# Graph network kernel on one core: x loaded in the first phase, attention sums moved to the tile tables, norm and window counts joined with the features of three blocks

## The chip, the cores and the metric

One core of one Trainium2 chip. The metric is the device time of one execution in microseconds (us); the lower the better. The profile is one execution of its own.

## The reference, cut to what matters

The input is x (3750 nodes by 256), a list of 63750 edges sorted by destination, with a source and one of 8 types each.

```python
h = maximum(layernorm(x), 0)
feat_all = einsum('ni,rhid->rnhd', h, conv_weights)      # 8 types, 4 heads, 64 columns
el = sum(feat_all[type, src] * attn_l[type], -1)         # one number for each edge and head
er = sum(feat_all[type, dst] * attn_r[type], -1)
e = leaky_relu(el + er)                                  # softmax of e over the edges of one destination
x = x + segment_sum(alpha * feat_all[type, src], dst) + h_bias
h = maximum(layernorm(x), 0)                             # then an input layer, and three layers of
h = relu(mean_over_neighbours(h) @ W_agg + h @ W_self + b_hid)
x = x + h @ W_out + b_out
```

## The kernel before, in words

All matrices are cut into blocks of 128 nodes (30 blocks) and chunks of 512 nodes (8 chunks). The program is a row of phases. Each phase is a `with nc.Block()` in which every engine has its own list of instructions, written out by hand, with semaphores between them; at the end of a phase all engines meet, and at some ends GpSimd also clears the semaphores of the phase (`end_phase`, L131). So no engine starts on a phase before the slowest list of the one before is through. SP's list holds most of the transfers, and is worked off in its order: a `wait_ge` in it holds back all that stands behind.

The phases that the change touches, in order:

- **Lists** (L325 to L388). SP loads the four edge lists (12 transfers), ACT's queue loads the attention vectors and the convolution weights (18 transfers), GpSimd and VectorE (DVE) set constants, and DVE turns the lists into numbers (L385).
- **Ends and checks** (L396 to L460, then a sort that is skipped for sorted edges). DVE decides whether the edges are sorted.
- **Tile tables** (`tile_tables`, L613). DVE works out what each group of 128 edges needs (L630 to L669), TensorE (PE) turns it, GpSimd makes masks (L691 to L697), ACT packs pairs of a code and a column for each edge into `pack` (L717, L719), and SP stores them as `pair_tab` (L708). A second copy of the phase is skipped here.
- **Counts** (L740). DVE compares the edges' codes with the starts of 240 windows of 16 nodes (L749 to L752), PE adds the hits up (L812 to L818), and DVE makes `edge_i` of the sums, the first edge of each window (L771 to L805). GpSimd makes 12 row masks beside it (L827 to L838), SP stores them (L857). SP also loads all of x into `x_all` (L844, L846), whose last rows DVE has zeroed (L743), and four small vectors (L848 to L851).
- **Attention and norm** (L889). DVE and GpSimd multiply the weights by the attention vectors (L914, L932) and DVE sums the products to `wlr` (L918). Then come the 8 chunks of the norm: DVE's statistics and scaling (L870 to L882), PE's turning (L972) and products with `wlr` (L961), ACT's relu (L948, L949), DVE's keeping of the results in `elr` (L897). SP meanwhile loads the pairs of the windows of ten blocks with `load_pairs`, and behind them stores `er_tab` (L988).
- **Windows and features** (from L1469). For each of 30 blocks PE makes 7 or 8 windows of the count matrix `a_tab` (three products each, L265, of operands that DVE makes at L254 and L255) and four feature products of 512 columns (each of four matmuls, L1325). ACT takes both out of PSUM (L273 and L1181, L1183); SP stores the windows (L279), ACT's queue the features (L1187). Of the 235 windows with nodes in them, block b takes `BLOCK_W[b]`. SP loads the pairs of block b + 10 ahead of the stores of block b, until all are loaded.

After that come the edge phase (gathers of features, about 530 to 1250 us) and the three layers (to the end). Neither is changed.

The load that matters in the prediction reads where each window begins from `edge_i`, which the counts phase has written:

```python
regs = starts_held[0:many]
sp.load(regs, edge_i[0:1, bass.ds(first, many)])
...
for k, at in enumerate(edge_starts(sp, FIRST_W[b], BLOCK_W[b])):
    sp.dma_start(pairs_in[:, FIRST_W[b] + k, :, :]...)
```

Of the kernel before, what the change touches and what calls it, by code (L numbers as in the profile page):

```python
# [23 lines left out]
FP32 = mybir.dt.float32  # L24
# [42 lines left out]
BLOCK_W = [NREAL * (b + 1) // NBLK - NREAL * b // NBLK for b in range(NBLK)]  # L67
# [32 lines left out]
def gnn_kernel(nc, x, src, dst, etype, conv_w, attn_l, attn_r, h_bias, w_in, b_in, w_agg, w_self,  # L100
               b_hid, w_out, b_out, out):
    ctx = ExitStack()
    with ctx:
        gat = ExitStack()
# [88 lines left out]
        rel = sb("rel", [P, 8, DEPTH])  # L193
        edge_i = sb("edge_i", [1, NTW], I32)
        lo_i = sb("lo_i", [1, NTW], I32)
        past_i = sb("past_i", [1, NTW + 1], I32)

# [41 lines left out]
        def shift_codes(dve, b):  # L239
# [7 lines left out]
            dve.wait_ge(s_rel, b + 1)  # L247
# [32 lines left out]

        def when(eng, flag):
# [27 lines left out]
        s_ld, s_xl, s_at = [nc.alloc_semaphore(a) for a in ("vectors_loaded", "all_x_loaded", "weights_in")]  # L309
        lists_i = stg[:, 5000:5000 + CQ + NTW].bitcast(I32)  # L310
        prod = [stg[:, 4096 + 2048 * i:4096 + 2048 * (i + 1)] for i in range(2)]

        def hrow(i):
            return hT[:, :, :].rearrange("p k n -> p (k n)")[:, i * T:(i + 1) * T].rearrange(
                "p (c j) -> p c j", c=CT)
# [7 lines left out]
        attn = [side[:, 2048 * i:2048 * (i + 1)] for i in range(2)]  # L325

        with nc.Block() as block:
            @block.sync
            def _(sp):
                sp.wait_ge(s_pad, 4)  # L330
                for a, buf in zip((dst, dst, src, etype), raw):
# [5 lines left out]
                                 a[E - rest:E].rearrange("(o j) -> o j", o=1)).then_inc(s_rl, 16)  # L337

# [131 lines left out]
        def sort_edges(flag, key_array, other_array):  # L470
# [18 lines left out]
            with nc.Block() as block:  # L489
# [42 lines left out]
                def _(dve):  # L532
                    with when(dve, flag):
                        for v, buf in zip((0, PADSRC, 0), raw_s):
                            dve.memset(buf, v).then_inc(s_z, 1)
# [76 lines left out]

        def tile_tables(c0, c1, flag=None):  # L613
# [11 lines left out]
            with nc.Block() as block:  # L625
                @block.vector
                def _(dve):
                    with when(dve, flag):
# [19 lines left out]
                        for i, to in enumerate((typ_t, dstloc, fidx_i, code_t, col_t)):  # L648
# [6 lines left out]
                            while at < c1 * P:  # L655
# [15 lines left out]
                                at = end  # L671

# [13 lines left out]
                def _(pool):  # L686
                    with when(pool, flag):
# [9 lines left out]
                        c.link(pool.tensor_copy(dst16[:, 0:nc_, :], cut(dstm)))  # L697

# [15 lines left out]
                def _(act):  # L714
                    with when(act, flag):
# [9 lines left out]
        s_w, s_wc, s_ws, s_ri, s_rw, s_xz = (sem("window_steps"), sem("windows_counted"), sem("window_sums"),  # L725
                                             sem("row_masks"), sem("row_masks_stored"), sem("x_zeroed"))
        begun = stg[:, 1792:1792 + CT * NTW].rearrange("p (c w) -> p c w", c=CT)
        PARTS_T = P // GRAIN
        room = hT[:, :, :].rearrange("p k n -> p (k n)")
# [6 lines left out]
        cbx = stg[0:1, 7800:7800 + NS * U].rearrange("p (s t) -> p s t", s=NS)  # L736
        cnx = work[0:1, 8192:8192 + NS * U].rearrange("p (s t) -> p s t", s=NS)
        subs_of = lambda a: a[0:1, 0:NS * U].rearrange("p (s t) -> p s t", s=NS)
        DUP = 14
        with nc.Block() as block:  # L740
            @block.vector
            def _(dve):
                dve.memset(x_all[:, NBLK - 1:32, :], 0.0).then_inc(s_xz, 1)  # L743
# [10 lines left out]
                same_t = stg[0:1, 8704:8704 + 512]  # L754
# [37 lines left out]
                row = stg[0:1, 8704:8704 + spots]  # L792
                below = stg[0:1, 8768:8768 + (NC - 1) * spots].rearrange("p (c j) -> p c j", c=NC - 1)
# [12 lines left out]

            @block.tensor
            def _(pe):
                for g in range(PARTS_T):
                    pe.wait_ge(s_w, g + 2)  # L810
                    for c in range(CT):
                        pe.matmul(PS[0:1, 7, 0:NTW], one_c, ended[:, g, c, :], start=(g == 0 and c == 0),  # L812
                                  stop=(g == PARTS_T - 1 and c == CT - 1))
                for c in range(CT):
                    pe.matmul(PS[0:1, 5, 0:NTW], one_c, ended[:, PARTS_T - 1, c, :], start=(c == 0), stop=(c == CT - 1))
                pe.wait_ge(s_w, PARTS_T + 3)
                for c in range(CT):
                    mm = pe.matmul(PS[0:1, 6, 0:NTW], ones[:, 0:1], begun[:, c, :], start=(c == 0),  # L818
                                   stop=(c == CT - 1))
                mm.then_inc(s_wc, 1)  # L820
# [18 lines left out]

            @block.sync  # L840
            def _(sp):
                sp.wait_ge(s_xz, 1)
                full = NBLK - 1
                sp.dma_start(x_all[:, 0:full, :],  # L844
                             x[0:full * P, :].rearrange("(b p) f -> p b f", p=P)).then_inc(s_xl, 16)
                sp.dma_start(x_all[0:N - full * P, full, :], x[full * P:N, :]).then_inc(s_xl, 16)  # L846
                for buf, v in ((hb_b, h_bias), (bout_b, b_out)):
                    sp.dma_start(buf[:, :], v.rearrange("(o n) -> o n", o=1).to_broadcast([P, F])).then_inc(s_ld, 16)  # L848
                sp.dma_start(bin_c[:, :], b_in.rearrange("(k p) -> p k", p=P),
                             allow_slow_non_contiguous=True).then_inc(s_ld, 16)  # L850
                sp.dma_start(bh_c[:, :, :], b_hid.rearrange("l (k p) -> p l k", p=P),  # L851
                             allow_slow_non_contiguous=True).then_inc(s_ld, 16)
                sp.wait_ge(s_ri, 12)
                at = 0
# [12 lines left out]
        def ln_stats(dve, rows, c, slot, stats_done, var_ready):  # L867

            for b in range(4):
                dve.bn_stats(stats[:, slot, b, :], rows(b)).then_inc(stats_done, 1)  # L870
# [1419 lines left out]
```

## Time and profile before

| | us |
|---|---|
| median of 3 runs | 2076.78 |
| lowest and highest | 2074.4, 2078.51 |
| the profiled execution | 2072.4 |
| its span, first to last instruction | 2070.6 |
| mean granted TensorE clock, as a share of full speed | 0.901 |

Over the span PE is busy 86%, ACT 55%, DVE 52%, GpSimd 25%. The span falls into the setup (to 154.5 us), the windows and features (to 530), the edges (to 1250) and the layers. Times of instructions are counted from the span's start.

In a timeline a row is: start, duration, engine, line, operation, what it writes and reads, count, and in brackets how long the engine was idle before and what ended that. "SPq" and "ACTq" rows are transfers being issued by a queue; their duration is that of issuing, not of moving the data.

### The profile page before, as it was taken

To read this page: it belongs to the slowest core of one execution; us is meant where nothing else is said; L and a number is where in the kernel's file an instruction comes from. 1 tells how busy PE (TensorE), PEld (TensorE's weight loads), DVE (VectorE), ACT (ScalarE), POOL (GpSimd) and SP (SyncE) were. 2 spreads that over 40 slices of the span, in tenths; PEclk is the share of its full clock that TensorE was granted. 3 is DMA by queue.
4 is the path that set the end of the run, shared out by engine and by line. 5 is a ranking of instruction groups with operands and counts; after the bars stand their busy time and mean duration, and the time that the engine had idled before them with its cause. 6 is when DMAs were issued, how large, how long until landed. Compare 5 with 4: busy or idle time off the path is not lost. (4 is left out here: it accounts for less than half of the span.)

```text
span 2070.6 us, 26209 instructions
## 1 busy us (share of the span) xinstructions
PE 1778.8 (86%) x7604; PEld 1236.5 (60%) x7605; DVE 1081.7 (52%) x3126; ACT 1143.4 (55%) x2498; POOL 521.1 (25%) x544
## 2 busy tenths in 40 slices
PE   1159999999497879798797955999989999999998
PEld 1054444444375557565575634777777777877777
DVE  4858888888365676766767535453550000301011
ACT  0034455565387779797787734454545444544442
POOL 2600000000577777777777300000000000000000
PEclk7569999999687789797898887999999999999999
DMA  4314555555655566565665325333324333363432
GB/s 129 82 14 152 171 195 192 181 201 199 202 146 161 152 182 176 153 188 159 171 173 161 101 63 181 99 123 107 110 77 128 113 116 112 98 208 123 135 123 62
DMA packets 285221, 290.67 MB, mean 140 GB/s; under 512 B 88673, under 2 KB 248102, under 8 KB 284806
## 3 DMA queue, kind: packets, MB, share of 16 engines
q1 hardware_dynamic: 235094, 186.23, 29.3%
q0 software_dynamic: 23952, 66.46, 12.1%
q10 hardware_dynamic: 26016, 36.15, 4.8%
q8 instruction: 64, 1.05, 0.2%
q14 instruction: 95, 0.78, 0.1%
HBM read 201.26 MB, written 87.48 MB: 139 GB/s over the span
## 5 line engine op out<-in xcount | busy, mean ns | idle before, releaser
L1141 POOL DMA_INDIRECT work<-feat_tab,fidx_i x499 | 477.6, 957 | 586.0 <-issue 581.2
L2117 PE MATMUL PS<-a_pe,y_hi 128*128 128x512 f32 (+2 forms) x1440 | 556.7, 392 | 33.4 <-ACT a_pe L2014 33.4
L2117 PE MATMUL PS<-a_pe,y_lo 128*128 128x512 f32 (+2 forms) x1440 | 536.7, 379 | 0.0
L2014 ACT ACTIVATE a_pe<-a_in 128x1536 fp32r<-128x1536 f16 (+1 forms) x240 | 329.3, 1376 | 342.7 <-PE PS L2117 329.1
L2117 PEld LDWEIGHTS PS<-a_pe,y_hi 128*128 128x128 f32 (+1 forms) x1440 | 274.0, 190 | 103.1 <-ACT a_pe L2014 35.0
L1210 ACT ACTIVATE work<-work 128x64 f32<-128x64 f32 x1344 | 325.1, 332 | 0.0
L2117 PEld LDWEIGHTS PS<-a_pe,y_lo 128*128 128x128 f32 (+1 forms) x1440 | 274.2, 190 | 55.2 <-issue 6.7
L1385 PE MATMUL PS<-work,stg 128*128 128x260 f32 x1008 | 289.6, 437 | 6.5 <-ACT work L1210 4.6
L1385 PEld LDWEIGHTS PS<-work,stg 128*128 128x128 f32 x1008 | 207.5, 217 | 65.0 <-issue 19.6
L255 DVE TENSOR_SCALAR side<-iota_c,work 128x512 f16<-128x512 f16 x705 | 245.8, 349 | 0.0
L1325 PE MATMUL PS<-wbuf,hT 128*128 128x512 f32 x480 | 226.9, 595 | 0.0
L2221 DVE TENSOR_TENSOR mean<-PS,rdeg 128x1024 f32<-128x1024 f32 (+1 forms) x24 | 27.2, 1135 | 363.3 <-PE PS L2117 363.0
L273 ACT ACTIVATE side<-PS 128x512 f16<-128x512 f32 x235 | 128.7, 595 | 142.0 <-PE PS L265 69.6
L254 DVE TENSOR_SCALAR side<-iota_c,rel 128x128 f16<-128x128 f16 x705 | 176.9, 251 | 49.1 <-PE PS L265 48.3
L265 PE MATMUL PS<-side 128*128 128x512 f16 x705 | 173.6, 381 | 24.6 <-DVE side L255 16.1
L265 PEld LDWEIGHTS PS<-side 128*128 128x128 f16 x705 | 68.3, 98 | 151.2 <-DVE side L255 36.1
L1335 PE MATMUL PS<-er_win,stg 128*128 128x32 f32 x1008 | 134.9, 294 | 22.5 <-ACT stg L1196 22.5
L1335 PEld LDWEIGHTS PS<-er_win,stg 128*128 128x128 f32 x1008 | 129.9, 211 | 26.4 <-ACT stg L1196 24.5
L1325 PEld LDWEIGHTS PS<-wbuf,hT 128*128 128x128 f32 x480 | 91.8, 191 | 75.1 <-issue 57.9
L1181 ACT ACTIVATE stg<-PS 128x512 f32<-128x512 f32 x120 | 72.0, 600 | 43.3 <-PE PS L1325 42.5
L1588 DVE TENSOR_TENSOR work<-work,PS 128x1024 f32<-128x1024 f32 x42 | 51.3, 1221 | 69.1 <-ACT work L1202 69.1
L1579 DVE TENSOR_TENSOR stg<-PS,dstloc 128x512 f32<-128x512 f32 x126 | 86.4, 686 | 1.5
(257 smaller groups left out, 1674.0 us busy)
## 6 DMA issues: line engine op xcount, KB each, us to landing
a_in<-a_tab SPq DMA_DIRECT2D x210, 384.0 KB, 3.2
feat_tab<-stg ACTq DMA_DIRECT2D x120, 260.0 KB, 2.2
a_tab<-side SPq DMA_DIRECT2D x235, 128.0 KB, 1.8
stg<-dst_tab SPq DMA_DIRECT2D x42, 384.0 KB, 4.0
work<-feat_tab,fidx_i POOLq DMA_INDIRECT x499
h_tab<-outs SPq DMA_DIRECT2D x42, 130.0 KB, 2.6
h_tab<-outs SPq DMA_DIRECT2D x8, 520.0 KB, 3.9
stg<-h_tab SPq DMA_DIRECT2D x8, 520.0 KB, 4.1
```

Of the source, the lines that this page charges most:

```text
L254: dve.tensor_scalar(code[:, s, :], iota_c[:, 0:P], rel[:, k, j:j + 1], None, ALU.is_equal)
L255: dve.tensor_scalar(other[:, s, :], iota_c[:, :], pairs_in[:, w, j, 1:2], None, ALU.is_equal).then_inc(built.pair, 1)
L265: pe.matmul(PS[:, BBS[w % len(BBS)], :], code[:, s, :], other[:, s, :], start=(j == 0), stop=(j == DEPTH - 1)).then_inc(built.free, 1)
L273: act.activation(counts[:, w % KEPT_W, :], PS[:, BBS[w % len(BBS)], :], ACT.Copy).then_inc(built.evicted, 1)
L1141: pool.indirect_dma_start(out=ring[:, s, 0:FE], out_offset=None, in_=feat_tab[:, :], in_offset=bass.IndirectOffsetOnAxis(ap=idx, axis=0)). ...
L1210: ins = act.activation(a, a, ACT.Copy, scale=ring[:, s, F + h:F + h + 1])
L1325: mm = pe.matmul(PS[:, cc, :], hT[:, k, b * P:(b + 1) * P], wc[:, k, cc * 512:(cc + 1) * 512], start=(k == 0), stop=(k == K2 - 1))
L1335: mm = pe.matmul(PS[:, ERB, u * RH:(u + 1) * RH], onehotT[:, u * P:(u + 1) * P], er_win[:, :], start=True, stop=True)
L1385: mm = pe.matmul(PS[:, OUTS[j], 0:EXT], onehot[:, t, :], ring[:, j * U + t, 0:EXT], start=(t == 0), stop=(t == U - 1), skip_group_check=True)
L1579: dve.tensor_tensor(onehot[:, q * QT:(q + 1) * QT, :], IOTA_PS.unsqueeze(1).to_broadcast([P, QT, P]), dstloc[:, tiles_of(i, j, q, QT)].uns ...
L2014: act.activation(a_pe[:, load % A_PE, :, 0:n], a_in[:, load % A_IN, :, 0:n], ACT.Copy).then_inc(s_conv, 1)
L2117: mm = pe.matmul(SUMS(ug, n)[:, f, :], y[0:rows_of, kb, f * P:(f + 1) * P], a_pe[0:rows_of, load % A_PE, kb % KB, 0:n], start=(kb == 0 and ...
```

## The change

x is loaded in the first phase behind the lists (`load_all_x`), with the four small vectors; the zeroing of its last rows goes there too. If the edges had to be sorted, x would be loaded again. The attention products and sums become the functions `attention_sums` and `attention_products`, called at the end of DVE's and GpSimd's lists in the tile tables. The index rows move from `hT` to a buffer of their own that is given back after the setup. The counts phase and the norm phase become one. In it DVE does the norm first and then the counts; PE does the norm, four feature products, the sums of the counts, eight feature products more; ACT does the norm and then keeps and stores the 12 feature products (three blocks, `AHEAD`). SP stores `er_tab`, then the row masks, then waits for a new semaphore that DVE raises at the end of the counts, and then loads the pairs of ten blocks. The windows are spread over the other 27 blocks, 8 or 9 each, 87 of them in the first ten.

```diff
+AHEAD = 3
+BLOCK_W = [0] * AHEAD + [NREAL * (b + 1) // (NBLK - AHEAD) - NREAL * b // (NBLK - AHEAD) for b in range(NBLK - AHEAD)]
...
+        def load_all_x(sp, turn=1):
+            sp.wait_ge(s_xz, turn)
+            sp.dma_start(x_all[:, 0:FULL, :], x[0:FULL * P, :]...).then_inc(s_xl, 16)
+            sp.dma_start(x_all[0:N - FULL * P, FULL, :], x[FULL * P:N, :]).then_inc(s_xl, 16)
...
 (first phase, SP, behind the 12 list transfers)
+                load_all_x(sp)
+                for buf, v in ((hb_b, h_bias), (bout_b, b_out)):
+                    sp.dma_start(buf[:, :], ...).then_inc(s_ld, 16)
+                sp.dma_start(bin_c[:, :], ...).then_inc(s_ld, 16)
+                sp.dma_start(bh_c[:, :, :], ...).then_inc(s_ld, 16)
...
 (first phase, DVE)
+                dve.memset(x_all[:, FULL:32, :], 0.0).then_inc(s_xz, 1)
...
 (tile tables, ends of DVE's and GpSimd's lists)
+                    if flag is None:
+                        attention_sums(dve)
...
+                    if flag is None:
+                        attention_products(pool)
...
+        def attention_sums(dve):
+            dve.wait_ge(s_at, 16 * (K2 * R + 2))
+            for i in range(2):
+                dve.tensor_tensor(prod[0], wc[:, 0, :], attn[i], ALU.mult).then_inc(s_pr, 1)
+                dve.wait_ge(s_pr, 3 * i + 1)
+                for k in range(K2):
+                    if k == 1:
+                        dve.wait_ge(s_pp, i + 1)
+                    dve.tensor_reduce(wlr[...], prod[k]..., AX.X, ALU.add).then_inc(s_pr, 1)
+                    dve.wait_ge(s_pr, 3 * i + k + 2)
+
+        def attention_products(pool):
+            pool.wait_ge(s_at, 16 * (K2 * R + 2))
+            for i in range(2):
+                if i == 1:
+                    pool.wait_ge(s_pr, 3)
+                pool.tensor_tensor(prod[1], wc[:, 1, :], attn[i], ALU.mult).then_inc(s_pp, 1)
...
 (the joined phase, DVE: the norm, then the counts)
+                with when(dve, 0):
+                    dve.memset(x_all[:, FULL:32, :], 0.0).then_inc(s_xz, 1)
+                dve.wait_ge(s_xr, 1)
+                ln_stats(dve, x_rows(0), 0, 0, s_bs, s_vr)
+                over_chunks(dve, step)
...
+                dve.sem_inc(s_wd, 1)
...
 (ACT, behind the norm)
+                act.wait_ge(s_ee, NC)
+                for q in range(4 * AHEAD):
+                    keep_features(act, q)
...
 (PE, behind the norm)
+                pe.wait_ge(s_ht, 2 * NC)
+                for cc in range(4):
+                    sum_features(pe, cc)
+                pe.wait_ge(s_ee, NC)
+                (the sums of the counts, as before)
+                for q in range(4, 4 * AHEAD):
+                    sum_features(pe, q)
...
 (SP)
                 sp.wait_ge(s_ld, 16 * 4)
+                sp.wait_ge(s_xl, 32)
+                with when(sp, 0):
+                    load_all_x(sp, 2)
+                    sp.wait_ge(s_xl, 64)
+                sp.sem_inc(s_xr, 1)
...
-                for b in range(EARLY):
-                    load_pairs(sp, b)
-                over_chunks(sp, store)
+                over_chunks(sp, store)
+                sp.wait_ge(s_ri, 12)
+                (12 stores to rm_tab, as before)
+                sp.wait_ge(s_rw, 16 * 3 * H)
+                sp.wait_ge(s_wd, 1)
+                for b in range(AHEAD, AHEAD + EARLY):
+                    load_pairs(sp, b)
                 sp.wait_ge(s_et, 16 * NC)
...
 (windows and features: DVE, PE, ACT and SP)
-                for b in range(NBLK):
+                for b in range(AHEAD, NBLK):
```

## Rows read from the trace of the kernel before

**Rows 1.** By stage: busy PE, PEld, DVE, ACT, POOL; granted clock, DMA share, GB/s.
```profile
83.20:154.50 71.30, 29.08 (x192) 28.14 (x192) 46.47 (x119) 18.47 (x25) 11.11 (x2) 0.62 0.13 11
157.50:530.00 372.50, 362.42 (x1185) 159.94 (x1185) 316.21 (x1438) 203.88 (x475) 0.00 (x0) 0.99 0.56 186
```

**Rows 2.** Timeline of the attention and norm phase, DVE, GpSimd and SP.
```profile
83.22 4.49 POOL L932 TENSOR_TENSOR stg<-wbuf,side 128x2048 f32<-128x2048 f32 x1 [10.26 <-POOLq L740]
83.23 6.63 DVE L914 TENSOR_TENSOR stg<-wbuf,side 128x2048 f32<-128x2048 f32 x1 [3.25 <-PEq L740]
84.76 58.85 SPq L228 DMA_DIRECT2D work<-pair_tab  x78
...
103.62 1.40 DVE L870 BATCH_NORM_STATS2 stats<-work 128x6 f32<-128x256 f32 x4
...
141.35 0.42 DVE L897 TENSOR_SCALAR stg<-PS 128x256 f32<-128x256 f32 x1 [1.36 <-PE PS L961]
143.66 5.61 SPq L988 DMA_DIRECT2D er_tab<-stg  x8
154.49 0.71 DVE L1470 MEMSET outs<- 128x780 f32 x1 [12.72 <-PEq L133]
```

**Rows 3.** Timeline of the first phase.
```profile
1.64 16.92 ACTq L346 DMA_DIRECT2D wbuf<-in_L_gnn_conv_weights  x16
...
8.99 1.01 SPq L336 DMA_DIRECT2D hT<-in_edge_type  x1
15.70 1.43 DVE L385 CAST hT<-hT 128x512 f32<-128x512 int32 x4 [12.14 <-DMA hT<-in_edge_type]
19.02 0.17 DVE L400 COPY small<-hT 128x7 f32<-128x7 f32 x1 [1.89 <-PEq L327]
```

**Rows 4.** Timeline of the tile tables and the counts.
```profile
43.01 0.68 POOL L697 CAST stg<-hT 128x512 int16<-128x512 f32 x1
...
52.10 0.70 DVE L743 MEMSET work<- 128x768 f32 x1 [2.08 <-PEq L625]
...
53.26 6.44 SPq L846 DMA_DIRECT2D work<-in_x  x1
...
60.12 3.24 POOL L832 TENSOR_TENSOR stg<-stg 1x814 f32<-1x814 f32 x1
...
62.00 1.39 DVE L751 TENSOR_SCALAR small<-hT 128x7 f32<-128x7 f32 x1
...
71.73 0.46 DVE L771 TENSOR_SCALAR stg<-PS,small 1x240 f32<-1x240 f32 x1
```

**Rows 5.** DMA engines' busy tenths in 40 slices: 0 to 25 us, then 50 to 75.
```profile
DMA  0029999998899999999999999799999970000000
...
DMA  0000013999999999999999999941000000000000
```

**Rows 6.** SP's pair loads: first and last of one burst, first of the next.
```profile
90.43 0.86 SPq L228 DMA_DIRECT2D work<-pair_tab  x2
...
94.05 0.33 SPq L228 DMA_DIRECT2D work<-pair_tab  x1
...
96.47 0.86 SPq L228 DMA_DIRECT2D work<-pair_tab  x2
```

**Rows 7.** Windows and features: PE's feature matmuls late in the phase.
```profile
499.79 1.45 PE L1325 MATMUL PS<-wbuf,hT 128*128 128x512 f32 x3
...
502.37 1.88 PE L1325 MATMUL PS<-wbuf,hT 128*128 128x512 f32 x4
...
505.39 1.88 PE L1325 MATMUL PS<-wbuf,hT 128*128 128x512 f32 x4
```

**Rows 8.** Windows and features: SP while it still loads pairs.
```profile
278.67 3.98 SPq L228 DMA_DIRECT2D work<-pair_tab  x8
282.69 6.09 SPq L279 DMA_DIRECT2D a_tab<-side  x8
289.94 4.35 SPq L228 DMA_DIRECT2D work<-pair_tab  x8
```

More of the change, by code:

```diff
@@ L103, in gnn_kernel @@
     with ctx:
-        gat = ExitStack()
+        gat, early = ExitStack(), ExitStack()
         def kept(name, shape, dt=FP32):
@@ L742, in _, with x_rows, keep, step @@
             def _(dve):
-                dve.memset(x_all[:, NBLK - 1:32, :], 0.0).then_inc(s_xz, 1)
+                def x_rows(c):
+                    return lambda b: x_all[:, bass.ds(c * 4 + b, 1), :].rearrange("p o f -> p (o f)")
+                def keep(c, slot):
+                    dve.wait_ge(s_el, c + 1)
+                    dve.tensor_scalar(elr[:, bass.ds(c * 4, 4), :, :],
+                                      PS[:, 4 + slot, 0:256].rearrange("p (b i n) -> p b i n", b=4, i=2),
+                                      0.0, None, ALU.add).then_inc(s_ee, 1)
+                def step(c, slot, first, last):
+                    if not last:
+                        ln_stats(dve, x_rows(c + 1), c + 1, 1 - slot, s_bs, s_vr)
+                    if not first:
+                        wait_past(dve, s_tp, c - 1)
+                    ln_finish(dve, x_rows(c), c, slot, s_sd, s_rs, s_hn, hN[:, slot, :, :])
+                    if not isinstance(c, int) or c > 1:
+                        keep(c - 2, slot)
+                with when(dve, 0):
[3 more added lines that the diff above has]
+                over_chunks(dve, step)
+                keep(NC - 2, 0)
+                keep(NC - 1, 1)
                 c = Chain(dve, s_w)
@@ L838, in _ @@
                 c.link(pool.tensor_scalar(cnx, cnx, BIG, None, ALU.mult))
[L840 to L854, printed above, removed]
-                for a, n in ((csx, U + 1), (cbx, U), (cnx, U)):
-                    for h in range(H):
-                        sp.dma_start(rm_tab[:, at:at + n].unsqueeze(0), a).then_inc(s_rw, 16)
-                        at += n
-                sp.wait_ge(s_rw, 16 * 3 * H)
@@ L979, in _ @@
                 halves(NC - 1, (NC - 1) % 2)
+                pe.wait_ge(s_ht, 2 * NC)
+                for cc in range(4):
+                    sum_features(pe, cc)
+                pe.wait_ge(s_ee, NC)
+                for g in range(PARTS_T):
+                    pe.wait_ge(s_w, g + 2)
+                    for c in range(CT):
+                        pe.matmul(PS[0:1, 7, 0:NTW], one_c, ended[:, g, c, :], start=(g == 0 and c == 0),
+                                  stop=(g == PARTS_T - 1 and c == CT - 1))
+                for c in range(CT):
+                    pe.matmul(PS[0:1, 5, 0:NTW], one_c, ended[:, PARTS_T - 1, c, :], start=(c == 0), stop=(c == CT - 1))
+                pe.wait_ge(s_w, PARTS_T + 3)
+                for c in range(CT):
+                    mm = pe.matmul(PS[0:1, 6, 0:NTW], ones[:, 0:1], begun[:, c, :], start=(c == 0),
+                                   stop=(c == CT - 1))
+                mm.then_inc(s_wc, 1)
+                for q in range(4, 4 * AHEAD):
+                    sum_features(pe, q)
             @block.sync
@@ L1484, in _ @@
                 w = 0
-                for b in range(NBLK):
+                for b in range(AHEAD, NBLK):
                     many = BLOCK_W[b]
@@ L1670, in _ @@
                 w = 0
-                for b in range(NBLK):
+                for b in range(AHEAD, NBLK):
                     if b + EARLY < NBLK:
```

195 lines of the change are left out of this document (81 added, 114 removed).

## The prediction

> **What bounds the kernel now.** I read the busy time by stage first. Windows and features run from 157.5 to 530 us with PE busy 362 of 372.5 us at the full granted clock, while DVE has 316 [rows 1]: there PE is the bound, and a feature product taken out gives its whole time back. The setup before is another thing. From 83.2 to 154.5 us no engine is busy for more than 47 of 71 us [rows 1]; it is a row of phases, and each is as long as its longest list. So I read the timeline of that phase next. DVE does the attention sums from 83.23 to 103.6 us and the norm from 103.62 to 141.77 us. SP, beside it, issues the 78 pair loads from 84.76 to 143.61 us and `er_tab` to 149.27 us, and the next phase begins at 154.49 us [rows 2]. The pair loads are as long as all that DVE does there, and are hidden behind it almost exactly. That is the point on which I forecast: the change puts them behind the counts, where nothing hides them.
>
> All steps are in the profiled execution's time. Its run took 2072.4 us (span 2070.6); the median of the runs shown is 4.4 us higher, and I add the sum of the changes to that median.
>
> **1. x in the first phase.** SP has issued its lists at 10.0 us, ACT's queue its weights at 18.6 us, and the next phase begins at 19.02 us [rows 3]. SP now also issues x, which alone took it some 0.4 + 6.44 us, held until about half was moved [rows 4, 5], and four vectors, which I put at 2.6 us (a window store takes 0.76, 6.09 us for eight [rows 8]). Undisturbed SP ends at 19.4 us, 0.8 after ACT: I call the low end +0.9. But the DMA engines are 90% busy until 20 us with lists and weights, and x alone keeps them so for 20 slices of 0.625 us, 12.5 us [rows 5]. If SP or ACT is held until all is moved, the phase ends 12.5 us later. Neither end is likely, since an issue waits for room, not for landing; I take the middle, +6.5. The lists stand ahead of x on its own queue, so I leave DVE's wait for them (to 15.7 us [rows 3]) alone. The Trainium skill (DMA: Bandwidth & Descriptors, section "Issuing engines are not separate DMA queues") says that transfers of all issuing engines interleave on the same 16 engines; taken to its end that is the +12.5 side. The zeroing of 0.70 us leaves the counts [rows 4] and hides behind the 12.1 us for which DVE waits for the lists [rows 3]: -0.6. x was hidden beside the counts before, so its early arrival gives nothing.
>
> **2. Attention beside the tile tables.** DVE's list is the long one of the tile tables: it ends at 50.02 us and the next phase begins 2.08 us later [rows 4]. The attention work is put at the end of that list. Before it took 20.4 us (83.23 to 103.62 [rows 2]), of which DVE waited 4.4 us: the product of 2048 columns took 6.63 us beside GpSimd's of 4.49 us, that is, it ran when GpSimd's was through. Now GpSimd can do its first product early, when its masks are through at 43.69 us [rows 4], while DVE still has L638 to do and all behind it. Would that hide 4.4 us? At 62.00 us a DVE operation on 7 columns took 1.39 us, to the end of a GpSimd operation on 814 that had begun at 60.12 [rows 4]. So GpSimd's early product should hold L638 up for as long as it saves later. I take 0 for the step (the 20.4 us move, none is saved), with -4.4 and +2 for the range. The Trainium skill (SBUF — State Buffer, section "SBUF: two separate sides") says that the two share a port pair as an exclusive lock, held for a whole instruction; without the lock the step would be worth -4.4.
>
> **3. One phase of two.** Between the last step of the counts and the attention product DVE was idle for 3.25 us [rows 2], for the row masks' landing and the meeting of the engines: gone, -3.3. New on DVE and SP is a test of a flag. Two ends of phases with such a test in one take 2.1 us after the tile tables [rows 4]; I take 1.5 us. Together -1.8.
>
> **4. What runs beside what.** GpSimd's 12 row masks ran beside the counts and held DVE up a few times, as above; now they run beside the norm. About 3 us leave the counts and I put 3 us into the norm: 0, with up to +6. PE does four feature products of 1.9 us at full clock (7.5 us) before the count sums; DVE needs those 19 us after it begins the counts (52.72 to 71.73 us [rows 4]), and the sums take PE some 10 us, so it is just in time: 0, up to +4 if the clock is low. ACT's 12 features at 3.0 us each [rows 7] are 36 us, over before SP's loads are. SP's `er_tab` stores, now taken as the norm goes, and the row masks (some 8 us) are over within the counts.
>
> **5. The pair loads.** Within a burst of eight the starts are 3.62 us apart for seven steps, 0.517 us each; to the next burst, after the register loads, it is 2.42 us [rows 6], 1.9 more than a step. The ten blocks now have 87 windows: 87 x 0.517 + 10 x 1.9 = 64.0 us, none of which can begin before DVE has written `edge_i` and raised the last semaphore. Before, from DVE's last step to the next phase was 12.7 us (141.77 to 154.49). Now it is 64.0 us and the end of the phase. From SP's last issue (149.27 us) to 154.49 us were 5.2 us [rows 2]; of these I put 1.3 us down to the landing of `er_tab`, which is long over now, and keep 3.9: 67.9 us. The step costs +55.2. In the windows phase the same loads come at the same pace (eight in 3.98 us [rows 8]), with DMA much busier, so the pace is that of issuing and I expect no gain from calm.
>
> Setup: 6.5 - 0.6 + 0 - 1.8 + 0 + 55.2 = +59.3.
>
> **6. Windows and features.** A feature product is four matmuls of 0.43 us (1.88 us for four less 1.45 us for three [rows 7]). Twelve products are gone: 48 x 0.43 = -20.6. The windows are as many as before. While SP still loads pairs, eight loads and eight stores have a period of 11.3 us (278.67 to 289.94 [rows 8]); PE's block with eight windows has 4 x 3.02 = 12.1 us [rows 7]. With nine windows SP needs 11.3 x 9/8 = 12.7 us and PE 12.1 + 0.6 (three matmuls at a sixth of 3.02 - 1.72 us each) = 12.7: SP comes level, and slips now and then. I take 0.25 us for each of 17 such blocks, +4, between 0 and +12.
>
> **Sum.** 59.3 - 20.6 + 4 = +42.7. The run of the profile would become 2115.1 us, the median 2119.5; I say **2119**. Less than 0.2% (4 us) cannot be told from no change.
>
> **The rivals.** First, a **milder** case: x is moved without holding anyone (+0.9 for +6.5), the early GpSimd product is really hidden (-4.4), and the windows, now denser, cost PE less than its rate, so that 27 blocks at 12.1 us stand in place of 30 (-36 for -16.6). That is 2090. For it speaks that ACT and DVE have room in a block; against it, that PE has none (it is busy for 362 of 372.5 us [rows 1]) and must still do 235 windows: chance 0.12. Second, a **worse** case: x holds the first phase to the end (+6), GpSimd's masks hold up the norm (+6), and SP becomes the bound of 17 blocks (+8): 2139, chance 0.18. Third, the **other side**, by one mechanism: the end of a phase need not hold the others. If PE, DVE and ACT went into the windows as soon as the pairs of the first block had landed, some 6 us of SP's 64 would be in the open and 58 less would be lost: 2061, faster. It decides when less than 21 us of the loads are exposed (64 less 43). Against it stand DVE's 12.72 us of idleness to 154.49 us, ended by the meeting of the phase after SP's last store [rows 2], and the single list in which SP stores windows behind these same loads: chance 0.04. The change may also not do what its words say in step 2, and by my sum it doesn't: the attention work moves to the end of the list that sets the tile tables' length, not into a shadow.
>
> **Numbers.** The forecast has 0.66, milder 0.12, worse 0.18, the other side 0.04. The forecast's own range takes in the steps' ends as they may add up: from 2119 - 5.6 - 4.4 - 4 = 2105 to 2119 + 6 + 2 + 8 = 2135. The 8 in 10 range reaches somewhat into both neighbours: 2097 to 2137. Slower by over 0.2%: 0.94. Within 0.2%, if between the mild case and the last one it meets in the middle: 0.02. Faster: 0.04.
>
> **What would show it.** In the profile after: the first phase ends at 20 to 31 us, L400 tells. The product of GpSimd starts near 50 us (43.7 + 6.5) and L638 waits for it. The last load of the ten blocks is issued some 64 us after DVE's last step of the counts, with every compute engine idle at the end; ten bursts of 8 or 9 at 0.52 us. The windows phase begins near 214 us and lasts some 356 us. The rest keeps its length. Loads at a pace under 0.3 us, or a windows phase that starts while they are issued, would prove me wrong; so would a windows phase under 340 us.

## The result, and the profile after

The change makes the kernel slower: 2131.2 us (median of 4 runs, 2124.33 to 2137.23) against 2075.6 (4 runs, 2073.25 to 2078.51), a ratio of 1.027 with a 95% interval of 1.0242 to 1.0298. Forecast were 2119 us, with a range of 2097 to 2137. The profiled execution took 2130.88 us, its span 2129.0 against 2070.6 before: 58.4 more.

Where the 58.4 us lie is read from where the phases begin. DVE's memset of `outs` opens the windows phase, the start of the last feature matmul closes it (the last number before the semicolon in these two rows of the view of one source line, first before and then after):

```profile
L1325 PE MATMUL PS<-wbuf,hT x480: 592/592/1061, 160.0 to 527.8; 128*128 128x512 f32 x160
...
L289 PE MATMUL PS<-wbuf,hT x480: 592/592/1061, 124.1 to 584.9; 128*128 128x512 f32 x160
```

| | before | after | difference | forecast |
|---|---|---|---|---|
| windows phase begins | 154.49 | 214.12 | +59.6 | +59.3 |
| its length | 373.3 | 370.8 | -2.5 | -16.6 |
| the rest of the span | 1542.8 | 1544.1 | +1.3 | 0 |

The setup came out at the forecast sum, and the windows did not. The timeline of the changed kernel's setup, all engines (it answers to [rows 2 to 4]):

```profile
1.65 26.69 ACTq L390 DMA_DIRECT2D wbuf<-in_L_gnn_conv_weights  x16
9.00 1.03 SPq L373 DMA_DIRECT2D index_rows<-in_edge_type  x1
10.51 12.26 SPq L362 DMA_DIRECT2D work<-in_x  x1
...
28.81 0.17 DVE L445 COPY small<-index_rows 128x7 f32<-128x7 f32 x1 [11.64 <-PEq L364]
...
53.55 4.82 POOL L676 TENSOR_TENSOR stg<-wbuf,side 128x2048 f32<-128x2048 f32 x1
54.05 4.60 DVE L703 TENSOR_SCALAR index_rows<-index_rows 128x512 f32<-128x512 f32 x1
...
64.00 2.29 DVE L662 TENSOR_TENSOR stg<-wbuf,side 128x2048 f32<-128x2048 f32 x1
...
77.73 2.29 DVE L667 TENSOR_REDUCE wlr<-stg 128x32 f32<-128x2048 f32 x1 [2.15 <-POOL stg L676]
82.95 1.40 DVE L816 BATCH_NORM_STATS2 stats<-work 128x6 f32<-128x256 f32 x4 [2.93 <-SPq L1021]
...
124.27 0.42 DVE L842 TENSOR_SCALAR elr<-PS 128x256 f32<-128x256 f32 x1 [1.36 <-PE PS L976]
...
147.28 0.14 DVE L925 COPY cuts_i<-turns_i 1x1 int32<-1x1 int32 x1
148.98 61.43 SPq L231 DMA_DIRECT2D work<-pair_tab  x87
214.12 0.71 DVE L1497 MEMSET outs<- 128x780 f32 x1 [66.70 <-PEq L134]
```

The last two rows are the change. SP begins to issue the 87 pair loads when DVE has ended the counts, needs 61.43 us for them, and DVE does nothing for 66.70 us where it was idle for 12.72 [rows 2]. The view by stage shows that hardly anybody else uses these 66 us (PE is busy for 4 of them, with the last early features), and that PE is no longer full in the windows phase (columns as in [rows 1]; the first stretch is norm and counts, the second the loads, the third windows and features, the last three 37 us each of the third):

```profile
82.90:147.50 64.60, 52.26 (x280) 39.36 (x281) 52.76 (x157) 23.52 (x43) 12.51 (x12) 0.81 0.16 42
147.50:214.00 66.50, 4.18 (x10) 1.52 (x8) 0.00 (x0) 2.05 (x6) 0.00 (x0) 0.56 0.14 20
217.00:585.00 368.00, 349.26 (x1137) 150.91 (x1137) 313.24 (x1435) 195.73 (x449) 0.00 (x0) 0.98 0.54 179
...
291.00:328.00 37.00, 33.20 (x102) 13.97 (x101) 27.52 (x127) 16.11 (x37) 0.00 (x0) 0.91 0.45 143
328.00:365.00 37.00, 34.52 (x111) 14.90 (x109) 30.20 (x140) 19.82 (x48) 0.00 (x0) 0.95 0.54 178
365.00:402.00 37.00, 32.47 (x102) 13.60 (x100) 28.49 (x132) 15.82 (x37) 0.00 (x0) 0.95 0.49 153
```

PE is idle for 2.5 to 4.5 us in each of these stretches of 37 us, and has a granted clock of 0.91 to 0.95 there, where the kernel before has 0.99 over the whole phase [rows 1]. Why is in the timeline of that phase, SP with ACT and PE beside it:

```profile
253.33 7.10 SPq L282 DMA_DIRECT2D a_tab<-side  x9
255.24 0.60 ACT L276 ACTIVATE side<-PS 128x512 f16<-128x512 f32 x1 [5.98 <-DMA a_tab<-side]
...
255.90 0.82 PE L268 MATMUL PS<-side 128*128 128x512 f16 x3 [1.74 <-ACT side L276]
...
263.22 3.98 SPq L231 DMA_DIRECT2D work<-pair_tab  x8
267.24 5.55 SPq L282 DMA_DIRECT2D a_tab<-side  x8
275.77 4.69 SPq L231 DMA_DIRECT2D work<-pair_tab  x9
280.51 7.10 SPq L282 DMA_DIRECT2D a_tab<-side  x9
...
299.86 1.46 PE L268 MATMUL PS<-side 128*128 128x512 f16 x3 [3.80 <-ACT side L276]
301.11 3.62 PE L289 MATMUL PS<-wbuf,hT 128*128 128x512 f32 x4
```

In front of a block's stores stand eight or nine loads, and before them the reading of as many registers. From the end of one round of stores to the next SP stores nothing for 6.8 us (260.43 to 267.24) and 7.7 us (272.79 to 280.51). Over the part of the phase in which SP still loads, SP's rows have 16 such pauses of 5.3 to 10.1 us, the middle one 7.6; the kernel before has 19 of 5.0 to 8.7 us, the middle one 6.8. There are four buffers for windows taken out of PSUM. While SP is at the loads no buffer comes free: ahead of the row at 255.24 ACT has waited 5.98 us for a store to land, and ahead of the one at 255.90 PE 1.74 us for ACT. The list of waits says how much that is over the whole phase (total us, times, longest), first before, from 157.5 to 528 us:

```profile
ACT side L273 <- DMA a_tab<-side: 58.8, 18, 6.1
...
PE PS L265 <- ACT side L273: 8.4, 9, 2.0
```

and after, from 217 to 585 us:

```profile
ACT side L276 <- DMA a_tab<-side: 72.0, 16, 8.1
...
PE PS L268 <- ACT side L276: 18.6, 11, 4.2
```

The last two rows of that timeline show a second cost. After a wait of 3.80 us PE's next feature product takes 3.62 us, where it otherwise takes 1.88 [rows 7]: the granted clock is down at its lower level of 1.2 GHz, 0.50 of full speed, for some us. Such a stretch follows each of PE's waits of 3.80, 2.48 and 4.24 us, and none of the other eight (1.96 us at most). In the kernel before, whose longest wait of this kind is 2.0 us, the granted clock is 1.00 from 165 to 528 us.

So in these waits the kernel before already lost something, and the changed one loses 10 us more by PE's row alone. That gave two questions. Is the +59.6 really the loads without their cover? And are the lost 14 us of the windows phase those of the burst in SP's list, or something else, such as a PE bound by windows?

### The profile page after: what moved, and what is told of

Same layout as the page of the kernel before. It is cut to its first block and busy times, and to the rows that moved or that the text cites. A ratio compares the mean times of both kernels' runs of the same rounds, so it can differ in the third digit from the quotient of the medians.

```text
span 2129.0 us, 26191 instructions
## 1 busy us (share of the span) xinstructions
PE 1778.2 (84%) x7604; PEld 1230.3 (58%) x7605; DVE 1079.2 (51%) x3123; ACT 1144.7 (54%) x2498; POOL 513.8 (24%) x544
## 5 line engine op out<-in xcount | busy, mean ns | idle before, releaser
L1412 PE MATMUL PS<-work,stg 128*128 128x260 f32 x1008 | 280.1, 426 | 10.8 <-ACT work L1243 8.5
L1412 PEld LDWEIGHTS PS<-work,stg 128*128 128x128 f32 x1008 | 200.6, 210 | 66.7 <-issue 17.8
L2248 DVE TENSOR_TENSOR mean<-PS,rdeg 128x1024 f32<-128x1024 f32 (+1 forms) x24 | 27.2, 1135 | 363.3 <-PE PS L2144 363.0
L289 PEld LDWEIGHTS PS<-wbuf,hT 128*128 128x128 f32 x480 | 93.3, 195 | 78.6 <-issue 64.5
```

What stands on the lines that cost most here:

```text
L289: mm = pe.matmul(PS[:, cc, :], hT[:, k, b * P:(b + 1) * P], wc[:, k, cc * 512:(cc + 1) * 512], start=(k == 0), stop=(k == K2 - 1))
L1412: mm = pe.matmul(PS[:, OUTS[j], 0:EXT], onehot[:, t, :], ring[:, j * U + t, 0:EXT], start=(t == 0), stop=(t == U - 1), skip_group_check=True)
```

## The experiments

Experiments 1 to 4 ran on a chip as fast as that of the runs above (the kernel before: 2074.36 us, 7 runs). Experiments 5 to 8 and experiment 9 ran on two other chips, where the kernel before takes 2260.47 and 2275.71 us (11 runs each). Setup and windows keep their lengths there, within a few us; the difference lies behind, in the edges and the layers. So between groups only the lengths of phases and the differences to the kernel before of the same chip are compared. Each change is against the changed kernel unless it says otherwise.

**1. The counts ahead of the norm.** If the missing cover is the cause, the loads must vanish behind the norm again.

```diff
 (the joined phase, DVE)
-                (the norm)
                 (the counts)
+                (the norm)
 (SP)
-                over_chunks(sp, store)
                 sp.wait_ge(s_ri, 12)
...
                 for b in range(AHEAD, AHEAD + EARLY):
                     load_pairs(sp, b)
+                over_chunks(sp, store)
 (PE: the sums of the counts, then the norm, then all 12 feature products)
```

> The changed kernel, with the counts ahead of the norm in the joined phase, so that the pair loads run beside the norm and er_tab is stored behind them. Theory (the loads behind the counts are exposed): DVE's counts and norm take 66 us from 81.8 us on, SP's loads (63 us) and the er_tab stores (6 us) begin at about 109, so the windows phase begins at about 183 us in place of 214, and the time is some 31 us under the changed kernel's: 2100. Rival (the loads cost what they cost wherever they stand, or the joined phase itself is slow): the windows phase begins within 5 us of 214. Second rival (the loads slow down beside the norm): they take over 70 us.

Measured: 2107.75 us (2099.81 to 2108.85), ratio 1.0171 (1.0146 to 1.0196). The loads run beside the norm, and the windows phase begins at 187.31 us instead of 214.12 (expected was 183; the loads began at 113, not at 109):

```profile
113.19 63.33 SPq L231 DMA_DIRECT2D work<-pair_tab  x87
176.58 5.63 SPq L1024 DMA_DIRECT2D er_tab<-elr  x8
```

The norm begins at 110.83 us and needs some 40 us, the loads 63: part stays in the open, and DVE is still idle for 36.43 us. The loads are hardly slower beside the norm (63.33 us against 61.43), and both rivals are out. The cover is worth 26.8 us. The windows phase, 372.5 us, is as poor as in the changed kernel.

**2. The loads on two queues.** The order stays, ten blocks alternately on SP and on ACT's queue.

```diff
-                for b in range(AHEAD, AHEAD + EARLY):
+                for b in range(AHEAD, AHEAD + EARLY, 2):
                     load_pairs(sp, b)
 (ACT, behind its 12 features)
+                act.wait_ge(s_rw, 16 * 3 * H)
+                act.wait_ge(s_wd, 1)
+                for b in range(AHEAD + 1, AHEAD + EARLY, 2):
+                    load_pairs(act, b)
```

> The changed kernel, with the pair loads of ten blocks shared by the queues of SP and ACT, every second block each. If what counts is the issuing on SP's list, the exposed 63 us become about 33 and the windows phase begins 30 us earlier, at 184: 2101. If the transfers themselves, or something that both queues share, set the pace, little is saved: under 10 us.

Measured: 2111.15 us (2105.26 to 2118.1), ratio 1.0197 (1.0161 to 1.0232).

```profile
151.25 30.14 SPq L231 DMA_DIRECT2D work<-pair_tab  x43
156.70 29.77 ACTq L231 DMA_DIRECT2D work<-pair_tab  x44
190.13 0.71 DVE L1501 MEMSET outs<- 128x780 f32 x1 [40.45 <-PEq L134]
```

Half of the loads take half of the time on each queue, at the same time. The loads are limited by the pace at which one queue issues them, 0.7 us each with the registers, and not by the moving of data. The phase begins 24.0 us earlier, 6 later than expected: ACT still had features to keep and began 5.5 us behind SP, and SP itself began 2.3 us later than in the changed kernel, since DVE ended the counts that much later.

**3. No early features.** `AHEAD = 0` takes the 12 products out of the setup and spreads the windows over 30 blocks again, 78 in the first ten.

```diff
-AHEAD = 3
+AHEAD = 0
 (PE, ahead of the sums of the counts)
-                for cc in range(4):
-                    sum_features(pe, cc)
```

> The changed kernel without the features of three blocks in the joined phase (AHEAD is 0): the windows go to 30 blocks again, and all 120 feature products stand in the windows phase. My first accounting (12 products are worth 20.6 us, denser windows cost 4): the setup ends 6 us earlier with 78 loads in place of 87, the windows phase is 16.6 us longer, so the time is 11 us over the changed kernel's. Theory after its trace (with 8 or 9 windows a block PE is held up for as long as the 12 products gave): the windows phase is as long as in the kernel before (373 us against 371), and the time is 3 to 5 us under the changed kernel's.

Measured: 2128.14 us (2124.66 to 2136.33), ratio 1.0281 (1.0248 to 1.0313). The windows phase begins at 210.78 us (nine loads fewer, 58.06 us for 78) and is 373.9 us long, as before the change. The changed kernel's, with 12 products fewer, has 370.8: they give back 3.1 us and not 20.6, so the first accounting is out. As a whole the two kernels cannot be told apart.

**4. The kernel before with the changed kernel's density.** The windows on the last 27 blocks, all 120 products in place, nothing else of the change.

```diff
-BLOCK_W = [NREAL * (b + 1) // NBLK - NREAL * b // NBLK for b in range(NBLK)]
+AHEAD = 3
+BLOCK_W = [0] * AHEAD + [NREAL * (b + 1) // (NBLK - AHEAD) - NREAL * b // (NBLK - AHEAD) for b in range(NBLK - AHEAD)]
...
 (SP, the loads of the setup; the loops over blocks of DVE and SP likewise)
-                for b in range(EARLY):
+                for b in range(AHEAD, AHEAD + EARLY):
```

> The kernel before, with its windows spread over the last 27 of the 30 blocks (8 or 9 each) and the first three blocks with features alone; nothing else is changed, PE's work is the same. Theory (SP's pair loads and stores do not keep up with 9 windows a block, and PE is held up behind the evictions): the windows phase grows from 373 to about 390 us; the 87 loads make the setup 5 us longer; the time is about 22 us over the kernel before. Rival (the density costs nothing, the lost time comes from elsewhere in the changed kernel): the windows phase stays within 4 us of 373, and the time within 9 us.

Measured: 2094.63 us (2087.36 to 2100.81), ratio 1.0116 (1.0084 to 1.0148). The phase begins at 157.61 us and lasts 389.1 us, 15.8 more than in the kernel before with the same work in it. The waits, 161 to 547 us:

```profile
ACT side L274 <- DMA a_tab<-side: 71.1, 14, 7.7
...
PE PS L266 <- ACT side L274: 19.8, 13, 3.8
```

They are those of the changed kernel (72.0 and 18.6). The density alone does it: of the 20.6 us that the products are worth it takes 15.8 here, and the changed kernel lost 18 of them. The rival is out. It remains to show what of the density hurts.

**5 and 6. One pair load behind each window store.** The same loads and stores, in another order in SP's list: no burst.

```diff
-                    if b + EARLY < NBLK:
-                        load_pairs(sp, b + EARLY)
+                    more = each_pair_load(sp, b + EARLY) if b + EARLY < NBLK else iter(())
                     for _ in range(BLOCK_W[b]):
                         window_sp(sp, w)
                         w += 1
+                        next(more, None)
+                    for _ in more:
+                        pass
```

`each_pair_load` is `load_pairs` as a generator: behind a block's first store it reads all the registers of the loads, and from then on it issues one load each time it is asked. Loads that are left when a block has no more stores go behind them.

In the changed kernel:

> The changed kernel, with one edit in the windows phase: SP issues one pair load behind each window store, in place of 8 or 9 loads in a row ahead of a block's stores. Theory (it is the burst of some 7 us on SP's list, with the reading of the registers, that keeps ACT and then PE waiting, and it is felt more with 9 windows a block): ACT's waits for a_tab stores (72 us) fall under 25, PE has no stalls left, and the windows phase is 345 to 352 us in place of 371; the time is 19 to 26 us under the changed kernel's. Rival (SP's total work of 12.7 us a block is the bound, in whatever order): the phase stays over 365 us.

In the kernel before:

> The kernel before with the same edit. Theory: the windows phase falls from 373 to about 362 us (PE's work of 358 us and a slow start), so the time is 10 us (0.5%) under the kernel before, and with e5 the 12 products are then worth the whole 20 us in the windows phase. Rival: within 3 us of the kernel before.

Measured, the changed kernel: 2293.06 us (2286.82 to 2297.58), ratio to the kernel before 1.0145 (1.0121 to 1.0169). It is 32.6 us over the kernel before of this chip, where the changed kernel was 55.6 over on its own: 23 us less, within the 19 to 26 expected. The windows phase has 343.9 us instead of 370.8, a little under the 345 to 352 expected. The wait is nearly gone (217 to 570 us):

```profile
ACT side L281 <- DMA a_tab<-side: 13.6, 13, 1.9
```

PE is full at full clock in the stretch where it lost most (first row below; the next two stretches of 37 us read 37.00 and 1.00 too). The other two rows are the whole phase but for its first us, first of this kernel and then of the changed one:

```profile
291.00:328.00 37.00, 37.00 (x126) 16.25 (x125) 33.94 (x157) 22.38 (x50) 0.00 (x0) 1.00 0.61 196
222.00:558.00 336.00, 336.00 (x1126) 147.78 (x1125) 307.75 (x1413) 198.20 (x447) 0.00 (x0) 1.00 0.59 195
...
222.00:585.00 363.00, 344.36 (x1127) 149.00 (x1125) 308.61 (x1413) 194.43 (x447) 0.00 (x0) 0.98 0.55 181
```

The same number of matmuls takes 363 us in the one and 336 in the other. Of the 27 us 18.6 are PE's idle time, all of it the waits for ACT, and 8.4 are longer busy time (344.4 against 336.0), most of it from the stretches at the lower clock that follow the three longest waits. So the waits cost nearly half as much again as their length here.

The kernel before: 2246.19 us (2241.32 to 2256.7), ratio 0.994 (0.9923 to 0.9957): 0.6% faster, a little more than the 0.5% expected. Its phase has 363.1 us instead of 373.3; ACT waits 4.0 us for `a_tab` instead of 58.8. Between these two, which differ in density and in the 12 products but have no burst, lie 363.1 - 343.9 = 19.2 us. That is the 20.6 of the forecast, nearly: the density costs next to nothing once the loads no longer stand in a block in front of the stores. While SP still loads, its pauses without a store are then 4.2 us at most in both. The rival of experiment 5 (over 365 us, with SP's sum as the bound) is out.

**7. x in the tile tables' phase.** SP loads x and the vectors behind the stores of the tile tables instead of in the first phase.

```diff
 (first phase, SP)
-                load_all_x(sp)
-                (the four vectors)
 (tile tables, SP, behind the store of pair_tab)
+                        if flag is None:
+                            load_all_x(sp)
+                            (the four vectors)
 (tile tables, DVE: the zeroing of x_all's last rows goes to the start of its list;
  joined phase, DVE and SP: the tests of a flag for a second load of x are gone)
```

> The changed kernel, with x and the four vectors loaded by SP behind the stores of the tile tables, and not in the first phase. Theory (the x load held the first phase by 9.8 us, ACT's and SP's queues both waiting for room): the first phase ends at 19.0 us again, the attention sums cover the load, and the windows phase begins 9 us earlier (205): 2122. Rival (the first phase is late for another reason, the lists' landing or the zeroing): it ends at 25 us or later as before. Third: the attention sums do not cover it, and the joined phase waits for x.

Measured: 2307.66 us (2304.77 to 2308.76), ratio 1.0213 (1.0193 to 1.0233).

```profile
19.36 0.17 DVE L437 COPY small<-index_rows 128x7 f32<-128x7 f32 x1 [1.65 <-PEq L364]
...
51.09 0.51 SPq L361 DMA_DIRECT2D work<-in_x  x1
51.63 7.13 SPq L362 DMA_DIRECT2D work<-in_x  x1
...
73.13 1.41 DVE L817 BATCH_NORM_STATS2 stats<-work 128x6 f32<-128x256 f32 x4 [1.81 <-SPq L1017]
```

The first phase ends at 19.4 us instead of 28.8, and the norm begins 9.8 us earlier (73.13 against 82.95). The 9.8 are 9.45 of the first phase and 1.1 of a shorter boundary ahead of the norm (1.81 us instead of 2.93; the tests of the flag are gone), less 0.7 for the zeroing in DVE's list. So x in the first phase cost 9.4 us; behind the tables' stores nobody waits for it. The rival (the first phase late for another reason) is out. The windows phase begins at 205.35 us.

**8. All attention products on DVE.** GpSimd's two products go to DVE, to see whether GpSimd's early one is paid for at L703.

```diff
                     if k == 1:
+                        dve.tensor_tensor(prod[1], wc[:, 1, :], attn[i], ALU.mult).then_inc(s_pp, 1)
                         dve.wait_ge(s_pp, i + 1)
...
-                        attention_products(pool)
```

> The changed kernel, with all four attention products on DVE and none on GpSimd. The tile tables took DVE 33.9 us with GpSimd's help, 4.6 us of it in one small operation that stood behind GpSimd's first product. Theory (the two do not overlap on these products, so GpSimd's share hides nothing): L703 takes 0.43 us again, the chain of the tile tables and sums takes 32 to 33 us, and the windows phase begins 1 to 2 us earlier. Rival (GpSimd's product hides a part of the work): the chain is 3 us longer or more.

Measured: 2317.95 us (2311.74 to 2321.76), ratio 1.0255 (1.0231 to 1.0278), close to the changed kernel's 1.027.

```profile
54.54 0.43 DVE L704 TENSOR_SCALAR index_rows<-index_rows 128x512 f32<-128x512 f32 x1
...
76.59 2.29 DVE L668 TENSOR_REDUCE wlr<-stg 128x32 f32<-128x2048 f32 x1
81.80 1.41 DVE L815 BATCH_NORM_STATS2 stats<-work 128x6 f32<-128x256 f32 x4 [2.93 <-SPq L1020]
```

The operation on 512 columns that took 4.60 us beside GpSimd's product takes 0.43 us without it. DVE now does two products more (4.6 us) and has still the shorter list, by 1.6 us (32.25 against 33.88). But the windows phase begins no earlier (215.06 us): norm and counts took 2.1 us longer (66.6 against 64.5). The rows of the norm's products for one chunk show where, first here and then in the changed kernel:

```profile
113.44 3.51 PE L975 MATMUL PS<-wlr,side 128*128 128x64 f32 x16
...
114.34 1.90 PE L976 MATMUL PS<-wlr,side 128*128 128x64 f32 x16
```

In the second half of the norm PE's granted clock was 0.74 here (106 to 125.6 us) and 1.00 there (107.9 to 124.6), and DVE waited 9.8 us for these products instead of 7.9. That is 1.9 of the 2.1 us. Why the clock was lower is not shown.

**9. A kernel put together from these.** Counts first; x at the start of the joined phase, beside the counts; the row masks stored from ACT's queue; attention sums between counts and norm, with GpSimd's product beside the counts; no early features (`AHEAD` is 0); the 78 loads shared between SP (54) and ACT's queue (24); loads and stores interleaved. Some scratch buffers move.

```diff
 (the joined phase, DVE: the counts first, then)
+                attention_sums(dve)
+                dve.wait_ge(s_xl, 32)
 (SP)
-                for b in range(AHEAD, AHEAD + EARLY):
+                for b in (0, 2, 4, 6, 7, 8, 9):
                     load_pairs(sp, b)
 (ACT, ahead of the norm)
+                (the 12 stores to rm_tab)
+                act.wait_ge(s_wd, 1)
+                for b in (1, 3, 5):
+                    load_pairs(act, b)
```

> A version made of what the runs showed. Counts and norm in one phase, the counts first; x and the vectors issued by SP at its start; the row masks stored from ACT's queue; the attention sums on DVE between counts and norm, with GpSimd's products beside the counts; the pair loads of ten blocks (78, no features ahead) shared by SP (seven blocks) and ACT (three) beside the attention sums and the norm; in the windows phase one pair load behind each window store. Theory: DVE's chain sets the joined phase, about 27 + 19 + 38 us from 52 us on, so the windows phase begins at about 143 us (154.5 in the kernel before), and lasts 362 to 364 us (373). The time is 18 to 22 us under the kernel before's (about 0.9%). Rival: ACT's share of the loads (18 us) holds up the norm, which it must start with its roots, and the windows phase begins at 150 us or later.

Measured: 2260.56 us (2253.18 to 2263.95), ratio 0.9922 (0.9906 to 0.9937): 0.8% faster than the kernel before.

```profile
86.52 40.38 SPq L231 DMA_DIRECT2D work<-pair_tab  x54
87.64 16.28 ACTq L231 DMA_DIRECT2D work<-pair_tab  x24
...
144.54 0.71 DVE L1494 MEMSET outs<- 128x780 f32 x1 [5.45 <-PEq L134]
```

The setup is 10.0 us shorter than before and so is the windows phase (363.3 us), as expected within 2 us. The time is 15.2 us lower and not 18 to 22. The interval of the ratio overlaps with that of experiment 6, which changes only SP's order; by these runs the one can't be called faster than the other.

All kernels side by side, as differences to the kernel before of the front (begin 154.49, length 373.3), beside the difference of the medians of each group:

| | begins | length | sum | medians |
|---|---|---|---|---|
| changed kernel | +59.6 | -2.5 | +57.1 | +55.6 |
| 1 counts first | +32.8 | -0.8 | +32.0 | +33.4 |
| 2 two queues | +35.6 | -3.1 | +32.5 | +36.8 |
| 3 no early features | +56.3 | +0.6 | +56.9 | +53.8 |
| 4 before, dense | +3.1 | +15.8 | +18.9 | +20.3 |
| 5 changed, interleaved | +60.3 | -29.4 | +30.9 | +32.6 |
| 6 before, interleaved | +0.6 | -10.2 | -9.6 | -14.3 |
| 7 x in tile tables | +50.9 | -3.6 | +47.3 | +47.2 |
| 8 products on DVE | +60.6 | -0.1 | +60.5 | +57.5 |
| 9 put together | -10.0 | -10.0 | -20.0 | -15.2 |

The sum of the two phases' differences gives each kernel's time within some 5 us, so no difference larger than that lies behind them.

## Why the prediction was right, and where not

The direction, the mechanism and the setup's sum were right; one term of step 6 was much too small. The change cost 55.6 us by the medians where the sum said 42.7, and nearly all of the difference is that term (14.1 us). That 2131.2 still lies within the range is owed to the width of the whole: step 6 missed by more than its own end allowed.

- **Step 5, the pair loads**, was the whole case. Forecast were 67.9 us from DVE's last step to the windows phase, measured 66.7, against 12.7 before: SP began 1.6 us after DVE's last step, which the forecast had at nothing, and the loads took 61.4 us instead of 64.0. Experiment 1 shows that it is the cover (26.8 us back when the norm stands beside the loads), experiment 2 that it is the pace of issuing. The rival by which engines would go on without SP is out: DVE stands still until the phase ends, PE and ACT once their last early features are done.
- **Step 1, x**: forecast +6.5 of 0.9 to 12.5, measured +9.8 (19.02 to 28.81), +9.4 by experiment 7. It lay nearer to the "held" end. SP took 12.26 us to issue x instead of 6.44, and ACT's queue 26.69 instead of 16.92 for its weights; ACT ended last. The lists were not late (DVE's wait ended where it did before). With x moved away (experiment 7) ACT's queue was through with its weights at 18.9 us again. The Trainium skill (DMA: Bandwidth & Descriptors, section "Issuing engines are not separate DMA queues") says that transfers run on the same 16 DMA engines and interleave, whichever engine starts them. The rows agree in kind: with x and the weights under way together, both queues took longer to issue. How long a queue is held when both are at work it does not say; the middle between two ends was a guess, and 3.3 us too low.
- **Step 2, attention**: forecast 0, measured -0.2: tile tables and attention took 33.9 us against 13.7 before plus the 20.4 that left the other phase. Both halves of the working are in the rows: with GpSimd's first product early, DVE's first took 2.29 us instead of 6.63, and L703 (L638 before) took 4.60 us instead of 0.43 beside GpSimd's product of 4.82 us; in experiment 8, without that product, it took 0.43 again. The Trainium skill (SBUF — State Buffer, section "SBUF: two separate sides") has an exclusive lock, held for a whole instruction, that would do this. The rows agree: L703 ends at 58.65 us, 0.3 after GpSimd's product.
- **Step 3, one phase of two**: forecast -1.8, measured -2.4 (2.93 us of boundary against 2.08 + 3.25).
- **Step 4, what runs beside what**: forecast 0. The norm took 3.6 us more (41.7 against 38.15; its first scalings ran beside GpSimd's masks) and the counts 4.4 less (22.8 against 27.25): -0.9 together.
- **The setup's sum** met the measured one to 0.3 us, and that is luck: x cost 3.3 us more than forecast, and attention, the boundary, step 4 and the loads together 2.9 less.
- **Step 6, the windows**: "SP comes level, and slips now and then. I take 0.25 us for each of 17 such blocks, +4, between 0 and +12". This is the step that failed. The phase got shorter by 2.5 us and not by 16.6; with the products at 20.6 the slips are 18 us, outside the step's own range. The premise was that PE, busy for 362 of 372.5 us, has no waits worth counting; but 8.4 us of it were waits for ACT already, and they grew to 18.6, with 8.4 us of slower matmuls on top. I compared rates: what SP and what PE need for a block of nine windows. But experiment 5 has the same loads, stores and registers in the same list, and PE is full; so SP's sum is no bound. What fits is how long SP stores nothing while it loads, against how long four buffers last. Before, the pause is 6.8 us, and four of eight windows in PE's 12.1 us of step 6 last 6.0, by estimate; after, it is 7.6 us, and four of nine windows in 12.7 us last 5.6. The burst as the cause is shown by experiments 5 and 6; the count of buffers in it is argued, since no run changed it. Experiments 3 and 4 show that the density takes back the products' gain, 5 and 6 that the burst is how: without it 19.2 us of the 20.6 are there. The worse rival had SP as the bound, at +8, and for the wrong reason.

## What to carry to other kernels

Before a list of transfers is moved, ask what it runs beside: 87 small loads are 61 us of one queue. Beside 58 us of sums and norm 78 of them cost nothing, beside the norm alone (40 us) part of them showed, and behind it they were paid in full. And where one queue both loads for later and stores for now, look at the length of its longest burst and at the buffers of those who wait for the stores, and not only at its sum against the block's time; laying the loads between the stores gave 10 us in the old kernel and 27 in the new.

## What was not expected of the hardware

- GpSimd's chain of 12 row masks took 14.4 us beside DVE's norm (81.81 to 96.24) and 21 us beside the counts before: the same operation on 814 columns took 1.53 us in the one and 3.24 in the other [rows 4]. DVE's scaling of four rows (L828) in turn took 3.35 and 2.80 us for the first two chunks, 1.38 once GpSimd was through. Which of the two engines was held up more differed between the two phases.
- Not every idle time lowers the clock. PE was idle for 3.8 us of the 37 from 254 to 291 us too, in spells of 1.9 us at most, and its granted clock was 1.00 there; the lower level came after the waits of 2.48 to 4.24 us. In the kernel before PE was idle for 8.3 us between 217 and 402 us, with a clock of 1.00.
- The kernel before took 9 to 10% more on the two other chips. By the profile of experiment 6 it lies behind the windows phase: the edges took some 820 us instead of 720, and the layers 916 instead of 820. Why is open.
